# Zeroing a finished part's semaphores inside of a later part, in a kernel of two transformer layers

## The reference

```python
x = x + _L0_attn_ref(_layernorm(x), ...)   # linear attention with decays, 32 heads of 128
#   qkv = silu(h @ qkv_w.T); a scan over blocks carries the state kv
#   return sigmoid(h @ gate_w.T) * (norm_w * rmsnorm(attn)) @ out_w.T
x = x + _L0_ffn_ref(_layernorm(x), ...)    # 512 -> 1376 -> 512, rank-16 additions to each weight
#   h1, h3 = lora(h, w1), lora(h, w3); return lora(silu(h1) * h3, w2)
x = x + _L1_attn_ref(_layernorm(x), ...)   # causal softmax attention with ALiBi, 32 heads of 16
#   q, k = layer_norm(q), layer_norm(k); softmax(q @ k.T * scale + bias) @ v @ w_out.T
x = x + _L1_ffn_ref(_layernorm(x), ...)    # gelu(h @ inter_w + inter_b) @ output_w + output_b, 2048 wide
return x
```

## Time and profile before

| | us |
|---|---|
| median of 3 executions (lowest, highest) | 1942.15 (1941.43, 1943.57) |
| the profiled execution | 1937.06 |
| its span, from the first to the last instruction | 1935.3 |
| TensorE busy in it | 1842.5 |
| VectorE, GpSimd, ScalarE busy | 1137.5, 986.4, 475.4 |
| last release of the meeting that ends ffn 1 | 1933.4 |

### The profile page before, as it was taken

One profiled execution on the slowest core, in us unless ns is written; L12 is line 12 of the kernel. 1 busy time (PEld: TensorE's weight loads), 2 busy tenths in 40 slices (PEclk: granted clock), 3 DMA queues, 4 the chain that ended last, 5 costly groups with the idle time before them and its releaser, 6 DMA issues. The chain is left out here.

```text
span 1935.3 us, 27511 instructions
## 1 busy us (share of the span) xinstructions
PE 1842.5 (95%) x10157; PEld 1445.1 (75%) x10157; DVE 1137.5 (59%) x1939; ACT 475.4 (25%) x623; POOL 986.4 (51%) x1148
## 2 busy tenths in 40 slices
PE   6999999999999999999999789998889999988998
PEld 5888888888888888888888568886654444357887
DVE  6674674874856747748747733304676888535601
ACT  4221111221211212112112120002414666633200
POOL 5676755755846657557535455444711121235432
PEclk9999999999999999999999899998987999899999
DMA  2111111111111111111101122202043333011112
GB/s 95 46 55 57 45 42 46 43 50 40 43 41 46 49 41 43 39 42 49 49 14 54 44 67 82 68 22 73 3 80 52 56 54 54 2 34 46 48 49 71
DMA packets 50501, 93.57 MB, mean 48 GB/s; under 512 B 8752, under 2 KB 13488, under 8 KB 50032
## 3 DMA queue, kind: packets, MB, share of 16 engines
q1 hardware_dynamic: 49776, 91.13, 17.3%
q10 hardware_dynamic: 640, 1.31, 0.4%
HBM read 76.15 MB, written 2.10 MB: 40 GB/s over the span
## 5 line engine op out<-in xcount | busy, mean ns | idle before, releaser
L366 POOL TENSOR_TENSOR a_w_l<-a_raw,a_w_h 128x1024 fp32r<-128x1024 f32 x96 | 205.6, 2141 | 8.0
L711 DVE TENSOR_TENSOR x<-x,a_ps 128x1024 f32<-128x1024 f32 x64 | 78.0, 1219 | 167.9 <-PE a_ps L165 167.9
L1596 ACT ACTIVATE a_pr<-a_ps 128x1024 f32<-128x1024 f32 (+1 forms) x192 | 153.3, 812 | 90.2 <-PE a_ps L1803 73.2
L1546 POOL TENSOR_SCALAR_AFFINE_SELECT a_pr<-a_pr 128x256 f32<-128x256 f32 x128 | 52.0, 406 | 217.0 <-ACT a_pr L1596 215.3
L1823 PE MATMUL a_ps<-a_K,a_Q 64*128 64x512 f32 (+2 forms) x384 | 136.5, 448 | 11.5 <-DVE a_mx L1702 8.8
L165 PE MATMUL a_ps<-a_tt_h,a_w_l 128*128 128x512 f32 x376 | 147.1, 391 | 0.0
L164 PE MATMUL a_ps<-a_tt_l,a_w_h 128*128 128x512 f32 x376 | 146.6, 390 | 0.0
L163 PE MATMUL a_ps<-a_tt_h,a_w_h 128*128 128x512 f32 x376 | 146.5, 390 | 0.0
L72 POOL TENSOR_TENSOR tick<-neg_half 128x1 f32<-128x1 f32 x120 | 35.0, 292 | 215.2 <-PE a_ps L165 208.1
L1698 DVE CUSTOM_DVE_ANT_0 a_masked<-a_ps,a_mask 128x384 bf16<-128x384 f32 (+3 forms) x256 | 115.0, 486 | 32.5 <-PE a_ps L1823 31.2
L1823 PEld LDWEIGHTS a_ps<-a_K,a_Q 64*128 64x128 f32 x384 | 66.7, 198 | 84.7 <-DVE a_mx L1702 33.4
(11 more groups left out here) (247 smaller groups left out, 4727.7 us busy)
## 6 DMA issues: line engine op xcount, KB each, us to landing
a_raw<-in_a_wpair SPq DMA_DIRECT2D x96, 256.0 KB, 2.7
f_raw<-in_f_w SPq DMA_DIRECT2D x33, 320.0 KB, 2.9
a_raw_s<-in_a_wout SPq DMA_DIRECT2D x32, 256.0 KB, 3.2
f_raw<-in_f_w SPq DMA_DIRECT2D x32, 256.0 KB, 2.6
a_raw_s<-in_a_wv SPq DMA_DIRECT2D x28, 256.0 KB, 2.6
a_cst<-in_a_cst SPq DMA_DIRECT2D x32, 129.0 KB
a_Q<-a_q_h SPq DMA_DIRECT2D x64, 64.0 KB
a_K<-a_k_h SPq DMA_DIRECT2D x54, 64.0 KB
```

The lines of the kernel that those rows point to most:

```text
L366: nc.gpsimd.tensor_tensor(to_l, src, to_h, ALU.subtract).then_inc(s(done), 1)
L711: nc.vector.tensor_tensor(a, a, units[i], ALU.add).then_inc(s("out_added"), 1)
L1546: nc.gpsimd.affine_select(tri, tri, [[0, 2], [1, P]], ALU.is_ge, 0.0, base=0, channel_multiplier=-1).then_inc(s("selected"), 1)
L1596: nc.scalar.activation(pr[n % SLOTS][:, 2 * i:2 * i + 2, 0:width], S[at % 2][:, :, skip:skip + width], ACT.Exp, scale=0.25).then_inc(s("sc ...
```

## The change

- `Sems` no longer hangs on the context; it can allocate a list of names at once.
- `clear` zeroes the numbers of one or more sets on GpSimd, a range of neighbours at a time. `release` gives them back without an instruction.
- Attention 0's semaphores that only its beginning uses are a set of their own, `s0` (35 names, `BEGIN`). GpSimd zeroes it near the end of attention 0, before `f0_split_a`, and it is released for ffn 0 to use.
- The other semaphores of attention 0 are zeroed in ffn 0, in GpSimd's loop at f = 3, and released behind that block.
- Those of ffn 0 and both blocks of attention 1 are zeroed in ffn 1, at the end of GpSimd's program.
- At the borders the zeroing and the meetings of line 90 are gone. Only ffn 1 zeroes its own set and meets, at the kernel's end.

```diff
-    def _clear(self):
-        self._nc.clear_and_free_semaphores(list(self._known.values()))
-        self._nc.all_engine_barrier()
+def clear(nc, *used):
+    numbers = sorted(h.num for sems in used for h in sems.handles())
+    first = 0
+    for i in range(1, len(numbers) + 1):
+        if i == len(numbers) or numbers[i] != numbers[i - 1] + 1:
+            nc.gpsimd.sem_clear(range(numbers[first], numbers[i - 1] + 1))
+            first = i
+
+def release(nc, *used):
+    for sems in used:
+        for handle in sems.handles():
+            nc.release_semaphore(handle)
...
+BEGIN = [f"x_in{t}" for t in range(NT)] + [f"first_v_in{k}" for k in range(KT)]
+BEGIN += [f"ln_{n}" for n in ("stats", "meanvar", "var_eps", "rstd", "shift", "normed", "transposed", "hi", "lo")]
+BEGIN += ["ident_in", "first_v_hi", "first_v", "v_first", "b11", "b12", "t1", "t2", "t3", "t_made", "t_hi", "t_lo",
+          "wg0_split", "wg0_hi"]
...
-        s = Sems(nc, ctx, "a0")
-        s2 = Sems(nc, ctx, "a0_next")
+        s0 = Sems(nc, "a0_begin", BEGIN)
+        s = Sems(nc, "a0")
+        s2 = Sems(nc, "a0_next")
...
             for i in range(2):
                 split_o(NG - 1, 2 + i, 4 * NG - 2)
+            clear(nc, s0)
             f0_split_a(nc, pool, s2, top)
...
+        release(nc, s0)
+    return s, s2
...
-def stage_ffn0(nc, top, a):
+def stage_ffn0(nc, top, a, past):
...
                 split(3, f)
                 if f <= 2:
                     split_w2(f - 1)
+                if f == 3:
+                    clear(nc, *past)
...
+        release(nc, *past)
+    return s, s2
...
-def stage_ffn1(nc, top, a, out_dram):
+def stage_ffn1(nc, top, a, out_dram, past):
...
                     nc.gpsimd.tensor_tensor(x[:, t, :], x[:, t, :], b2[:, :], ALU.add).then_inc(s("b2_added"), 1)
+            clear(nc, *past)
...
+    nc.clear_and_free_semaphores(s.handles())
+    nc.all_engine_barrier()
...
+        of_attention0 = stage_attention0(nc, top, a)
+        of_ffn0 = stage_ffn0(nc, top, a, of_attention0)
+        of_attention1 = stage_attention1(nc, top, a)
+        stage_ffn1(nc, top, a, out, of_ffn0 + of_attention1)
```

More of the change, by code:

```diff
@@ L75, with __init__ @@
 class Sems:
-    def __init__(self, nc, ctx, stage):
+    def __init__(self, nc, stage, names=()):
         self._nc, self._stage, self._known = nc, stage, {}
-        ctx.callback(self._clear)
+        for name in names:
+            self(name)
     def __call__(self, name):
@@ L85, in __call__, with handles @@
         return self._known[name]
-    def _clear(self):
-        self._nc.clear_and_free_semaphores(list(self._known.values()))
-        self._nc.all_engine_barrier()
+    def handles(self):
+        return list(self._known.values())
+def clear(nc, *used):
[13 more added lines that the diff above has]
+          "wg0_split", "wg0_hi"]
 def ln_vector(nc, dve, s, b, tiles, x_ready=None, after=None):
@@ L393, in split_pair @@
                 take_wait(nc, top, p)
-                both(w_h[:, 0:A12], w_l[:, 0:A12], raw[:, 0:A12], "wx_ready", "wx_hi", p)
+                both(w_h[:, 0:A12], w_l[:, 0:A12], raw[:, 0:A12], s("wx_ready"), s("wx_hi"), p)
                 if plain_ahead:
@@ L399, in split_pair @@
                 take_wait(nc, top, p)
-                both(w_h[:, A12:WP], w_l[:, A12:WP], raw[:, A12:WP], "wy_ready", "wy_hi", p)
+                both(w_h[:, A12:WP], w_l[:, A12:WP], raw[:, A12:WP], s("wy_ready"), s("wy_hi"), p)
             def split_v(g, k, loaded):
@@ L407, in split_v @@
                 take_wait(nc, top, n)
-                both(wv_h[:, k, :], wv_l[:, k, :], raw_s[:, k % 2, :], "wv_ready", "wv_hi", n - 2)
+                both(wv_h[:, k, :], wv_l[:, k, :], raw_s[:, k % 2, :], s("wv_ready"), s("wv_hi"), n - 2)
             def split_o(g, j, loaded):
@@ L416, in split_o @@
                 take_wait(nc, top, m)
-                both(o_h[:, j % 2, :], o_l[:, j % 2, :], raw_s[:, j % 2, :], "o_ready", "o_hi", m)
-            ln_gpsimd(nc, pool, s, b, TO, TO[0])
+                both(o_h[:, j % 2, :], o_l[:, j % 2, :], raw_s[:, j % 2, :], s("o_ready"), s("o_hi"), m)
+            ln_gpsimd(nc, pool, s0, b, TO, TO[0])
             for k in (2, 3):
-                pool.wait_ge(s(f"first_v_in{k}"), 16)
-                both(wv_h[:, k, :], wv_l[:, k, :], first_v[k], "wv_ready", "wv_hi", k - 2)
-                ln_gpsimd(nc, pool, s, b, TO, TO[k - 1])
+                pool.wait_ge(s0(f"first_v_in{k}"), 16)
+                both(wv_h[:, k, :], wv_l[:, k, :], first_v[k], s("wv_ready"), s("wv_hi"), k - 2)
+                ln_gpsimd(nc, pool, s0, b, TO, TO[k - 1])
             for t in TO[3:5]:
-                ln_gpsimd(nc, pool, s, b, TO, t)
+                ln_gpsimd(nc, pool, s0, b, TO, t)
             pool.wait_ge(s("raw_s_in1"), 16)
-            both(o_h[:, 0, :], o_l[:, 0, :], raw_s[:, 1, :], "wg0_split", "wg0_hi", 0)
+            both(o_h[:, 0, :], o_l[:, 0, :], raw_s[:, 1, :], s0("wg0_split"), s0("wg0_hi"), 0)
             for t in TO[5:]:
-                ln_gpsimd(nc, pool, s, b, TO, t)
+                ln_gpsimd(nc, pool, s0, b, TO, t)
             add_weights(0, 0)
@@ L614, in differences @@
                 t1, t2, t3, t4 = [to[:, 256 * n:256 * (n + 1)] for n in range(4)]
[L615 to L625, removed]
+                nc.vector.tensor_copy(t4, one[:, 0:256]).then_inc(s0("b11"), 1)
+                nc.vector.tensor_copy(t3, two[:, 0:256]).then_inc(s0("b12"), 1)
+                dve.wait_ge(s0("b12"), i + 1)
+                nc.vector.tensor_tensor(t1, t3, t4, ALU.subtract).then_inc(s0("t1"), 1)
+                nc.vector.tensor_tensor(t3, two[:, 256:512], t3, ALU.subtract).then_inc(s0("t3"), 1)
+                dve.wait_ge(s0("t1"), i + 1)
+                nc.vector.tensor_tensor(t2, two[:, 256:512], t1, ALU.subtract).then_inc(s0("t2"), 1)
+                dve.wait_ge(s0("t2"), i + 1)
+                nc.vector.tensor_tensor(t4, one[:, 256:512], t2, ALU.subtract).then_inc(s0("t_made"), 1)
+            ln_vector(nc, dve, s0, b, TO, lambda t: dve.wait_ge(s0(f"x_in{t}"), 16), differences)
             t_low(3)
@@ L959, in _ @@
                         mm.then_inc(s("v_made"), 1)
-                ln_tensor(nc, pe, s, b, TO, TO[2:4][k:k + 1])
+                ln_tensor(nc, pe, s0, b, TO, TO[2:4][k:k + 1])
             for i in range(2, NT):
                 if 4 <= i + 2 < NT:
-                    pe.wait_ge(s("t_made"), (i + 2 - 4) // 2 + 1)
-                    ln_tensor(nc, pe, s, b, TO, (TO[i + 2],))
-                pe.wait_ge(s("ln_lo"), i + 1)
+                    pe.wait_ge(s0("t_made"), (i + 2 - 4) // 2 + 1)
+                    ln_tensor(nc, pe, s0, b, TO, (TO[i + 2],))
+                pe.wait_ge(s0("ln_lo"), i + 1)
                 if i >= 4:
-                    pe.wait_ge(s("v_first"), i - 3)
+                    pe.wait_ge(s0("v_first"), i - 3)
                 project_v(TO[i], i % 4).then_inc(s("v_made"), 1)
-            pe.wait_ge(s("wg0_split"), 1)
-            pe.wait_ge(s("v_first"), 7)
+            pe.wait_ge(s0("wg0_split"), 1)
+            pe.wait_ge(s0("v_first"), 7)
             plain(o_h[:, 0, :], o_l[:, 0, :], [0, P, 2 * P, 3 * P])
-            pe.wait_ge(s("t_lo"), 4)
+            pe.wait_ge(s0("t_lo"), 4)
             for j in range(G4):
@@ L1269, in stage_attention1 @@
     with ctx:
-        attn = attention1_heads(nc, top, ctx, a)
-        attention1_out(nc, top, attn, a["a1_wout"], a["f1_w1"])
+        attn, heads = attention1_heads(nc, top, ctx, a)
+        out = attention1_out(nc, top, attn, a["a1_wout"], a["f1_w1"])
+    return heads + out
 R = 8
@@ L1943, in _ @@
             output(QUADS - 1, 1)
-    return attn
+    return attn, (qs, s)
 def f1_split(nc, pool, s, top, n, first):
@@ L2204, in program @@
                 top.update({f"f1_w_{n}": under(f"f1_w_{n}", [P, 2, 512], F32R) for n in "hl"})
-        stage_attention0(nc, top, a)
-        stage_ffn0(nc, top, a)
-        stage_attention1(nc, top, a)
-        stage_ffn1(nc, top, a, out)
+        of_attention0 = stage_attention0(nc, top, a)
+        of_ffn0 = stage_ffn0(nc, top, a, of_attention0)
+        of_attention1 = stage_attention1(nc, top, a)
+        stage_ffn1(nc, top, a, out, of_ffn0 + of_attention1)
 def decays():
```

63 lines of the change are left out of this document (32 added, 31 removed).

## The result

In the comparison made for the result the changed kernel took 1925.74 us (median of 4 executions, 1923.28 to 1928.39), the kernel before 1941.79 (4 executions, 1939.11 to 1943.57): ratio 0.9925, 95% interval 0.9912 to 0.9938, so 14.6 us less by the ratio and 16.1 by the medians. Three later comparisons of the same two gave ratios of 0.9943, 0.9917 and 0.9922, that is 11 to 16 us. Taken together, 49 executions of the kernel before have a mean of 1939.5 us and 21 of the changed kernel 1925.4 us, 14.1 us less. The forecast was 14.9 us less, at 1927.3 us; the range held the result.

The account below looks back on a forecast made before the run. TensorE, busy for 95% of the span, was taken as the bound, so only its standstills or clock pay. Savings of 12.65 + 0.75 + 0 + 1.5 = 14.9 us off 1942.15 gave 1927.3 us, range 1922 to 1932.5.

Parts of the forecast that it names:

- What goes: At the four borders between parts, only the block's end meeting is left: 2.8, 2.8, 4.3 and 2.75 us saved, sum 12.65.
- The end: At the kernel's end, ffn 1 zeroes its semaphores in 5 ranges instead of 10, at 0.15 us each: 0.75 us less.
- What is added: GpSimd's zeroings inside attention 0, ffn 0 and ffn 1 are hidden by waits or spare time: cost 0.
- The clock: TensorE's granted clock behind borders two and four may rise, giving 1.5 and 2.2 us; 1.5 us taken in all.
- 2.2 us of that would reach the end: At border four, a full clock makes the first product 2.6 us shorter, 2.2 of it before ScalarE's first normalised tile.
- one of the signs that I named: In the profile after, the granted clock would be at 1.00 for the transposes behind the heads.
- rival 1: At the borders, the next part's instructions come late; half of each saving given back makes 1935 us; chance 0.07.
- rivals 2 and 3: Heads' half-clock stretch goes entirely, 1915 us, chance 0.05 (borders' clock alone: 1925); or it grows, 1947.6 us, chance 0.02.
- Rival 4: Zeroings inside the parts hold up a queue, or the block's meeting gets longer: 1931 us, chance 0.03.

Follow-up runs that it names:

- Experiments 2 to 5: Changed kernel with, at its borders: two bare meetings each, 1930.10 us; merged zeroing, 1929.16; as many ranges as before with DRAINs, 1934.73; those without DRAINs, 1931.66.
- experiments 6 and 7: Changed kernel with attention 0's 87 semaphores zeroed one by one in ffn 0, 1925.97 us; the same with all zeroed twice, 1930.10 us.
- experiment 7: Changed kernel with attention 0's 87 semaphores zeroed one by one and all twice in ffn 0, 174 instructions: 1930.10 us.
- experiment 4: Changed kernel with all zeroing back at the borders in 10, 10, 21 and 10 ranges, a DRAIN ahead of each, one meeting behind: 1934.73 us.
- experiment 1: The changed kernel repeated unaltered three times: 1928.04, 1923.90 and 1922.28 us, ratios to the kernel before 0.9943, 0.9917 and 0.9922.

## Why the prediction was right

| step of the prediction | said, us | measured in the profile, us |
|---|---|---|
| four borders | 12.65 | 12.6 |
| the end, 5 ranges | 0.75 | 0.7 |
| zeroings inside the parts | 0 | 0 |
| the clock | 1.5 | 0.4 for all parts together |
| sum | 14.9 | 13.7 |

**What goes** was right to a tenth at each border, because it was read from the gap itself (release to first work, less 0.1) and not added up from instructions. Experiments 2 to 5 and the rows of line 89 say what the gap was made of, which I hadn't worked out: meetings 2.6 us, ranges some 5, DRAINs some 5. I had taken a range as 0.15 to 0.2 us. That was a range and its DRAIN; bare it is 0.07. The number of ranges alone doesn't set the length either: border four had 15 of them in 2.86 us, border one 10 in 2.89.

**The end** had 5 ranges, as the order of the numbers gave them, at 0.15 us each with its DRAIN.

**What is added** cost nothing. Attention 0's zeroing of 35 numbers stands at 1075.8 under a subtraction, and the six ranges of ffn 1 end at 1907.9, 12 us ahead of the block's end. The 87 numbers of ffn 0 take 0.501 us under line 205's, and the wait before the next split is still 2.86 us, the same as in the earlier trace rows:

```profile
1165.75 1.61 POOL L205 TENSOR_TENSOR f_w_l<-f_raw,f_w_h 128x512 fp32r<-128x512 f32 x1
1170.22 0.73 POOL L66 TENSOR_SCALAR f_w_h<-f_raw 128x640 fp32r<-128x640 f32 x1 [2.86 <-PE f_ps L1237]
```

The prediction's cover was too small (2.86 us; experiments 6 and 7 show 7.8), and its price without cover too high, since it counted ranges as GpSimd's time. Both errors pointed the safe way.

**The clock** is the term that was mis-sized. In the profile after, the mechanism at border four happened: the first product at full clock, 2.2 us shorter. The step that failed is "2.2 us of that would reach the end": the start of the next products came 1.75 us earlier against the border, and then 1.2 us went again, because the clock fell 9 us later in place of at once. And two of the three repetitions don't have that mechanism at all; their first product is as slow as before. Border two, from which I hoped for something too, kept its slow stretch (1328.2 for 6.8 us; before 1331.2 for 6.8). Nor did one of the signs that I named come: in the profile after, the clock falls behind the heads at 1700.3, and most of the transposes there run at 0.50. That costs nothing (the output part takes 32.60 us, 32.67 before), as I had said of border three. The parts of the changed kernel together took 1919.97 us, and 1923.5, 1922.3 and 1919.95 in the repetitions; the one profile of before has 1920.39. A gain from the clock of 1.5 us can't be seen in that, nor ruled out. The means of all executions, 14.1 us apart, leave 0.8 us beside the 13.3 of borders and end, with an uncertainty of more than 1 us.

**Rivals.** Code that comes late (rival 1) didn't happen: TensorE's first work stands 0.11 us behind the last release at every border of the changed kernel and of the experiments, and VectorE's first work follows after 0.10 us at borders one and four and 0.4 us at border two (at border three it waits for ScalarE's result). The Trainium skill (Runtime: NRT & Kernel Launch, Instruction fetch mechanics) would have a fetch behind a branch to code that isn't held; no run here shows one at these borders. The heads' slow stretch (rivals 2 and 3) kept its length, 41.0 us in both kernels. Rival 4, zeroings that hold up a queue, needs more than 7.8 us of them at the place in ffn 0 (experiment 7); the change has 0.5.

**The level.** I took the sum off the median of the three executions shown, 1942.15, and by the profile's 13.7 us that would be 1928.5. The medians of before lay at 1938 to 1942 and of after at 1922 to 1928, from 11.1 to 16.1 us apart; the uncertainty of the level was larger than that of any term but the clock, as the prediction had it. That 1927.3 came within 1.6 us of the 1925.74 measured is in part luck: another comparison gave 1922.28, at the edge of the range.

## What to carry to other kernels

Where all engines stand between two parts, price the gap as release of the last needed meeting to first work, and then look at what fills it: here a few long ranges without DRAINs, with one meeting behind them, already bring back 9.7 of the 12.6 us, and moving the zeroing into a busy part brings the last 2.9. The cover for an instruction in an engine's queue is its idle time plus the running operation of that engine ahead of it plus the slack of whoever waits for the next one; a longer version of the added piece, and then a doubled one, measures it. A gain in TensorE's clock right behind a pause shouldn't be counted in full: follow the work to the next wait, where it may fall again, and look at more than one profile: the gain was there in two of four.

## What the runs showed of the hardware

- Zeroing costs by instruction and by number: one number 0.044 us, 35 numbers 0.225, 87 numbers 0.501, 122 numbers 0.699, which is 0.04 us and 5.4 ns a number. Single ones follow at 0.074 us.
- They run in GpSimd's queue beside its computing: 0.501 us of zeroing under a subtraction left the next operation where it was.
- A DRAIN ahead of each range costs 0.07 to 0.09 us with nothing to drain (0.07 from its start to the range's in experiment 4, 0.09 in the kernel before); a bare meeting of five engines 0.33 us.
- TensorE's granted clock can stay at half for 41 us, and for 65 us with added work, with TensorE busy for 95 and 99% of it. The same code is at 1.00 in one execution and at 0.52 in another (experiment 1). Executions of the changed kernel took 1928.0 to 1930.7 us at a mean clock of 0.974, and 1922.3 to 1923.9 at 0.979.
